# Graph-network kernel on one core: adjacency loads of 2 KB runs over half the row blocks, all from SyncE

## Chip, cores and metric

One core of one Trainium2 chip runs the program. The metric is device time in microseconds (us) of one execution.

## What is computed

`x` is 4096 x 128, `adj` 4096 x 4096 (float32). Two layers are applied; only the parts that matter here are kept:

```python
h = relu(layernorm(x))
# layer 1: z = lap_mul(adj, h) @ W1 + b1, leaky relu; S = exp(-dist(z, z) / 2), 4 best per row kept
#          out = lap_mul(S + adj, h) @ W2 + b2        with lap_mul(A, v) = d * (A @ (d * v)), d = 1/sqrt(rowsum(A))
x = x + out
h = relu(layernorm(x))
# layer 2: x @ Wself.T + (adj @ h) @ Wneigh.T + b
x = x + out2
```

So `adj` (64 MB) multiplies a 4096 x 128 matrix three times: in layer 1 for `z` and again for the output, and in layer 2.

## The kernel before

**Stages.** The first pass over `adj` (to about 504 us) yields row sums and the first product. The distance stage follows (to about 826 us): 16 pairs of row tiles, each with matmuls into eight PSUM banks, key stores to DRAM by SyncE (L411), searches on VectorE, and GpSimd gathers of candidates. The second pass forms `(S + adj)` times the scaled `h` (to about 1158 us). The third pass forms `adj @ h` of layer 2.

**Tiling of passes two and three.** `adj` is cut into 8 groups of rows. A group's rows are 16 row blocks `m` of 32 rows `r`; its 4096 columns are four quarters `q` of 1024. Quarter `q` sits in partitions 32q to 32q+31, one row `r` per partition. The buffer `araw` has 4 slots of 16 KB per partition. Slot `c` takes chunk `c` of a group: 256 columns of each quarter, all 16 row blocks, 2 MB, through four DMAs of 512 KB, one for each quarter. Each DMA moves 512 runs of 1 KB (`load`, L351). A chunk holds 2 of the group's 8 units; a unit is 128 columns of every quarter.

For unit `j`, VectorE transposes 128 x 2048 elements of `araw` in 32 x 32 blocks into `tr[j % 4]` (`product_unit` L1013, instruction at L844), and TensorE multiplies that (L1275): 4 float32 matmuls of 512 columns, which the trace lists as 8. A `tr` buffer is written again when the unit four places earlier was used (semaphore `t_used`), or, for even units of the third pass, split (`lo_done`).

**Third pass.** Odd units go as before. Even units are split into a high and a low part: ScalarE writes the high part of the unit (`split_high`, L780), GpSimd subtracts it (`split_low`, L594), and TensorE then makes 12 matmuls (L1313). TensorE takes the units in order 0 to 7, except in the third pass's group 0, which has no splits and takes even units first (L1342).

**What is woven in.** For each group of the second pass VectorE has three pieces of work: `finish_second_a` of the group before (L1045: adds the gathered rows, layer norm statistics) after unit 6, `finish_second_b` after unit 7, `finish_second_c` of two groups before after unit 3. TensorE does `finish_second_b` after unit 0, `_c` after unit 1, `_a` after unit 2 (L1294). In the third pass VectorE does `finish_third` (L1100) of the group before after unit 3, when TensorE has done its part after unit 0. ScalarE evacuates a group's sum (L729) and stores its result with 4 DMAs (L774) between the splits.

**Who loads.** SyncE issues quarters 0 and 1 (`LOW`, `load_group` L438), ScalarE quarters 2 and 3 (`HIGH`, `load_high` L731, `load_third` L782), among its other instructions. Each issue waits until the slot's units of the group before are transposed (`load_chunk`, L381). The first group's four chunks are issued by SyncE alone, all quarters in the order 0, 1, 2, 3: chunks 0 and 1 between key stores of the distance stage (L422), chunks 2 and 3 at its end (L430, L432). GpSimd gathers 16 x 64 KB per group in the second pass (L553).

Of the kernel before, what the change touches and what calls it, by code (L numbers as in the profile page):

```python
# [41 lines left out]
CHUNKS = GROUPS // CHUNK_UNITS  # L42
SLOTS = 4
# [6 lines left out]
def gnn_kernel(nc, x, adj, W1, b1, W2, b2, W, b, out):  # L50
# [3 lines left out]
    adj_v = adj.rearrange("(m g r) (q c) -> q r g m c", m=QD * U, g=GROUPS, q=QD)  # L54

# [10 lines left out]
    with ctx:  # L66
# [49 lines left out]

        xs_g = xs[:].rearrange("p (u g) f -> p g u f", g=GROUPS)
# [273 lines left out]
        def _(sp):  # L391
# [28 lines left out]
            for n in range(SLOTS // 2):  # L420
                keys_store(1 + n)
                load(sp, n, 0, n * CHUNK_COLS, CHUNK_COLS, ALL)  # L422
# [7 lines left out]
            load(sp, 2, 0, 2 * CHUNK_COLS, CHUNK_COLS, ALL)  # L430
            sp.wait_ge(max_done, TILES // 2)
            load(sp, 3, 0, 3 * CHUNK_COLS, CHUNK_COLS, ALL)  # L432
# [11 lines left out]
            with sp.Fori(1, GROUPS + 1) as g2:  # L444
                load_group(g2)
# [154 lines left out]
        def _(act):  # L600
# [136 lines left out]
            def finish_second(g, last_chunk=True):  # L737
                act.wait_ge(var_ready, g + 2)
                act.activation(tmp32[:, 0:U], tmp32[:, 0:U], ACT.Sqrt).then_inc(sd_done, 1)
                if last_chunk:  # L740
                    load_high(g + 2, 3)
                act.wait_ge(kept, g + 1)
                act.wait_ge(zt_mm, g + GROUPS)
                wait_alone(act, z_done, g + (GROUPS + 1))
                for u in range(U):
                    ins = act.activation(z_st[:, u], xs[:, bass.ds(g + GROUPS * u, 1), :].rearrange("p o f -> p (o f)"), ACT.Relu,
                                         bias=negmr[:, u:u + 1], scale=tmp32[:, u:u + 1])
                ins.then_inc(h2_done, 1)
                act.wait_ge(zt_mm, g + (GROUPS + 1))
                act.wait_ge(q_mm, g + GROUPS)  # L750
                act.activation(flat(t_st[:]), ps_t, ACT.Copy).then_inc(zt_ev, 1)

            def group_second(g, i):
                load_high(g + 1, 0, 1, 2)
                finish_second(g - 1)
                evacuate(g, i, USED1, GROUPS)

            load_high(1, 0, 1, 2, 3)
# [7 lines left out]
            finish_second(GROUPS - 1, False)  # L766
            load_high(GROUPS + 1, 0, 1, 2, 3)
# [8 lines left out]
            def split_high(g, j):  # L776

                act.wait_ge(t_used, g * GROUPS + (USED1 + UNITS + j - 3))
                wait_alone(act, t_ready, g * GROUPS + (UNITS1 + UNITS + j + 1))
                act.activation(tr_hi[:, j // 2 % 2], tr[:, j % TSLOTS], ACT.Copy).then_inc(hi_done, 1)  # L780

            def load_third(g, c):  # L782

                eng_g = g + 1 if isinstance(g, int) else act.snap(g + 1)
                load_chunk(act, g + (GROUPS + 1), eng_g, c, HIGH)

            def group_third(g, i, loads=True):
                split_high(g, 0)
                split_high(g, 2)
                if loads:  # L790
                    load_third(g, 0)
                evacuate(g - 1, 1 - i, USED1 + UNITS, 2 * GROUPS)
                split_high(g, 4)
                if loads:
                    load_third(g, 1)
                store(g - 1, 1 - i)
                split_high(g, 6)
                if loads:
                    load_third(g, 2)
                    load_third(g, 3)  # L800
# [7 lines left out]
            group_third(GROUPS - 1, 1, False)  # L808
# [4 lines left out]
        def _(v):  # L813
# [199 lines left out]
            def product_unit(g, j, base_group, base_unit, place=None, slot_split=None):  # L1013

                place = j if place is None else place
                c, half = divmod(j, CHUNK_UNITS)
                if half == 0:
                    v.wait_ge(a_in[c], (g + base_group + 1) * PER_LOAD + loads_in[c])
# [4 lines left out]
                transposed(tr[:, place % TSLOTS], c, half * UNIT_COLS, U).then_inc(t_ready, 1)  # L1023


            for j in range(2):
                product_unit(0, j, 0, USED1)
# [84 lines left out]
            def group_third(g, i, prev):  # L1112
                for j in range(GROUPS):
                    after_split = j % 2 == 0 and not (isinstance(g, int) and j < TSLOTS)
                    product_unit(g, j, GROUPS, USED1 + UNITS, slot_split=split_units(g, j) - 1 if after_split else None)
                    if j == 2 and isinstance(g, int):
                        finish_second_c(GROUPS - 1)
                    if j == 3:
                        finish_third(prev, 1 - i)
# [7 lines left out]
            for place, j in enumerate(EVENS_FIRST):  # L1127
                product_unit(0, j, GROUPS, USED1 + UNITS, place)
# [13 lines left out]
        def _(pe):  # L1142
# [128 lines left out]
            def unit(g, j, bank, base_unit, src):  # L1271

                pe.wait_ge(t_ready, g * GROUPS + (base_unit + j + 1))
# [20 lines left out]
            def group_second(g, i, prev, before):  # L1294
                pe.wait_ge(acc_read, g + (2 * GROUPS - 2))
                for j in range(GROUPS):
                    if isinstance(g, int) and g == 0:
                        pe.wait_ge(y_ready, GROUPS + j + 1)
                    unit(g, j, i, UNITS1, ys)
# [22 lines left out]
            def group_third(g, i, prev):  # L1322
                pe.wait_ge(acc_read, g + (3 * GROUPS - 2))
                for j in range(GROUPS):
                    if j % 2 == 0:
                        split_unit(g, j, i)
                    else:
                        unit(g, j, i, UNITS1 + UNITS, hs)
# [13 lines left out]
            for place, j in enumerate(EVENS_FIRST):  # L1342
                pe.wait_ge(t_ready, UNITS1 + UNITS + place + 1)
# [41 lines left out]
```

## Time and profile before

| | us |
|---|---|
| median of 3 runs | 1495.37 |
| lowest, highest | 1486.2, 1497.4 |
| the profiled execution | 1488.5 |
| its span in the trace | 1486.7 |

The profiled execution is 6.9 us under the median of the runs, and its span leaves out 1.8 us around it. Times in the rows below are microseconds from the span's start. A line such as `DVE tr L844` is VectorE (DVE), the tensor written, and the code line; ACT is ScalarE, POOL GpSimd, PE TensorE; a `q` behind an engine is its queue or sequencer, as in `SPq` for SyncE. A float32 matmul stands as two in the counts.

### The profile page before, as it was taken

To read this page: it belongs to the slowest core of one execution; us is meant where nothing else is said; L and a number is where in the kernel's file an instruction comes from. 1 tells how busy PE (TensorE), PEld (TensorE's weight loads), DVE (VectorE), ACT (ScalarE), POOL (GpSimd) and SP (SyncE) were. 2 spreads that over 40 slices of the span, in tenths; PEclk is the share of its full clock that TensorE was granted. 3 is DMA by queue.
4 is the path that set the end of the run, shared out by engine and by line. 5 is a ranking of instruction groups with operands and counts; after the bars stand their busy time and mean duration, and the time that the engine had idled before them with its cause. 6 is when DMAs were issued, how large, how long until landed. Compare 5 with 4: busy or idle time off the path is not lost.

```text
span 1486.7 us, 12333 instructions
## 1 busy us (share of the span) xinstructions
PE 1065.4 (72%) x3170; PEld 609.4 (41%) x3170; DVE 871.5 (59%) x888; ACT 406.9 (27%) x997; POOL 475.3 (32%) x572
## 2 busy tenths in 40 slices
PE   0315556689787887899994778878697637878687
PEld 0202222334343366677773333433243314545444
DVE  1514553566655557799997737666465625545453
ACT  0534433554221054455552000000000102222131
POOL 1101111114121023344443175445344014535354
PEclk9956667899899988999997898989799877989899
DMA  9999999999999497443346899999999499999992
GB/s 191 189 222 198 224 211 195 202 223 196 183 198 220 101 217 169 158 168 144 134 174 148 194 237 241 211 248 236 201 253 219 102 206 218 261 230 226 210 232 52
DMA packets 254467, 291.36 MB, mean 196 GB/s; under 512 B 21600, under 2 KB 231520, under 8 KB 254432
## 3 DMA queue, kind: packets, MB, share of 16 engines
q1 hardware_dynamic: 161888, 162.49, 47.5%
q10 hardware_dynamic: 72576, 67.12, 20.1%
q0 software_dynamic: 19968, 61.36, 18.7%
q8 instruction: 13, 0.21, 0.1%
q14 instruction: 22, 0.18, 0.0%
HBM read 251.07 MB, written 39.85 MB: 196 GB/s over the span
## 4 chain that ended last, share of the span: by engine, by line
DMA 19%; DVE 14%; PE 11%; issue 8%; SPq 7%; ACTq 6%; POOL 4%; ACT 2%; DVEq 1%; POOLq 0%
DMA araw<-in_adj_dram 17%; SPq L358 7%; ACTq L358 4%; DVE tr L844 4%; POOL sq_rows L594 2%; PE ps L1313 2%; DVE m L987 2%; ACTq L774 2%; DVE i L989 2%; DVE bmax L974 2%; DMA t_st<-keys_scratch,block_row 2%; DVE out_t L1054 1%; PE ps L1257 1%; PE ps L1275 1%; PE ps L1260 1%
## 5 line engine op out<-in xcount | busy, mean ns | idle before, releaser
L844 DVE STREAM_TRANSPOSE tr<-araw 128x2048 f32<-128x2048 f32 (+3 forms) x244 | 441.6, 1839 | 363.4 <-DMA araw<-in_adj_dram 259.3
L1275 PE MATMUL ps<-tr,ys 128*128 128x512 f32 x512 | 256.2, 658 | 93.6 <-DVE tr L844 55.6
L1164 PE MATMUL ps<-tr,ys 128*128 128x512 f32 x448 | 236.7, 678 | 103.3 <-DVE tr L844 103.3
L358 POOL DMA_DIRECT2D araw<-in_adj_dram x120 | 77.7, 652 | 402.0 <-DVE tr L844 233.7
L1275 PEld LDWEIGHTS ps<-tr,ys 128*128 128x128 f32 x512 | 105.7, 213 | 230.0 <-issue 173.5
L1164 PEld LDWEIGHTS ps<-tr,ys 128*128 128x128 f32 x448 | 93.4, 218 | 221.4 <-issue 144.3
L705 ACT ACTIVATE araw<-ps,nsq 128x1024 f32<-128x1024 f32 x128 | 142.7, 1117 | 128.7 <-PE ps L1260 97.9
L594 POOL TENSOR_TENSOR sq_rows<-tr,zt_lo 128x2048 fp32r<-128x2048 f32 x28 | 126.8, 4536 | 158.2 <-ACT zt_lo L780 158.2
L553 POOL DMA_INDIRECT zt_lo<-neighbour_table,idx_st x128 | 129.8, 1014 | 46.0 <-issue 41.1
L627 ACT ACTIVATE ps<-araw 128x256 f32<-128x256 f32 x304 | 111.1, 366 | 61.4 <-DMA araw<-in_adj_dram 60.9
L1257 PE MATMUL ps<-sq_rows,pick 128*128 128x512 f32 x256 | 103.9, 406 | 26.2 <-POOL zs_lo L470 17.9
L1313 PE MATMUL ps<-sq_rows,zt_hi 128*128 128x512 f32 x112 | 56.8, 507 | 73.9 <-POOL sq_rows L594 73.8
L780 ACT ACTIVATE zt_lo<-tr 128x2048 fp32r<-128x2048 f32 x28 | 53.2, 1912 | 195.6 <-issue 96.4
L1258 PE MATMUL ps<-zt_lo,zs_hi 128*128 128x512 f32 x256 | 102.1, 399 | 0.0
L1259 PE MATMUL ps<-zt_hi,zs_lo 128*128 128x512 f32 x256 | 102.1, 399 | 0.0
L1260 PE MATMUL ps<-zt_hi,zs_hi 128*128 128x512 f32 x256 | 102.1, 399 | 0.0
L1275 PE MATMUL ps<-tr,hs 128*128 128x512 f32 x224 | 100.8, 592 | 0.0
L869 DVE TENSOR_REDUCE part<-araw 128x16 f32<-128x4096 f32 x13 | 57.5, 4420 | 71.8 <-DMA araw<-in_adj_dram 71.8
L1313 PE MATMUL ps<-zt_lo,zt_hi 128*128 128x512 f32 x224 | 81.4, 449 | 0.0
L987 DVE MAX8 m<-araw 128x8 f32<-128x4096 f32 x16 | 70.9, 4430 | 9.3 <-ACT araw L705 8.8
L482 POOL DMA_INDIRECT t_st<-keys_scratch,block_row x64 | 66.6, 1041 | 30.0 <-issue 24.7
L989 DVE FIND_INDEX8 i<-m,araw 128x8 uint32<-128x4096 f32 x16 | 70.7, 4419 | 0.0
(138 smaller groups left out, 1043.8 us busy)
## 6 DMA issues: line engine op xcount, KB each, us to landing
araw<-in_adj_dram SPq DMA_DIRECT2D x200, 512.0 KB
araw<-in_adj_dram ACTq DMA_DIRECT2D x120, 512.0 KB
araw<-in_adj_dram POOLq DMA_DIRECT2D x64, 512.0 KB, 16.0
keys_scratch<-araw SPq DMA_DIRECT2D x64, 512.0 KB, 3.6
xs<-in_x_dram SPq DMA_DIRECT2D x8, 512.0 KB, 7.7
araw<-in_adj_dram POOLq DMA_DIRECT2D x16, 256.0 KB, 8.9
araw<-in_adj_dram SPq DMA_DIRECT2D x16, 256.0 KB
araw<-in_adj_dram POOLq DMA_DIRECT2D x8, 448.0 KB, 10.6
```

What stands on the lines that cost most here:

```text
L358: eng.dma_start(araw[R * q:R * q + R, slot, :, at:at + cols], src).then_inc(landed[slot], DMA)
L553: gp.indirect_dma_start(out=gath[:, i, u, k, :], out_offset=None, in_=table, in_offset=bass.IndirectOffsetOnAxis(ap=idx_st[:, i, u * TOPK ...
L594: gp.tensor_tensor(tr_lo[:, i], tr[:, j % TSLOTS], tr_hi[:, i].bitcast(F32), ALU.subtract).then_inc(lo_done, 1)
L627: act.activation(junk[(m // 2) % 2][:, m % 2 * CHUNK_COLS:(m % 2 + 1) * CHUNK_COLS], araw[:, c, m], ACT.Copy, accum_out=part[:, g % 2, c, ...
L705: act.activation(keys[par][:, c * 1024:c * 1024 + 1024], ps[:, 2 * c:2 * c + 2].rearrange("p a b -> p (a b)"), ACT.Identity, bias=nsq[:, b ...
L844: return v.transpose(out.rearrange("p t (m s) -> p t m s", s=R), src)
L1164: pe.matmul(acc[bank], ys[:, c * GROUPS + first + i], ring1[:, (k + i) % RING1], start=start and i == 0, stop=stop and i == tiles - 1).the ...
L1257: pe.matmul(ps[:, c], pick[:], sq, start=True, stop=False)
L1258: pe.matmul(ps[:, c], zs_hi[:, par], zl, start=False, stop=False)
L1260: ins = pe.matmul(ps[:, c], zs_hi[:, par], zh, start=False, stop=True)
L1275: ins = pe.matmul(acc[bank], src[:, j * U + i], tr[:, j % TSLOTS, i], start=j == 0 and i == 0, stop=j == GROUPS - 1 and i == U - 1)
L1313: ins = pe.matmul(acc[bank], y[:, i, j // 2], t[:, half, i], start=j == 0 and i == 0 and n == 0, stop=False)
```

## The change

In passes two and three slot `n = 2w + h` now takes column half `w` (512 columns of each quarter, units 4w to 4w+3) and row-block half `h` (8 of the 16 row blocks). A slot still holds 2 MB in four DMAs of 512 KB, but each DMA has 256 runs of 2 KB. A unit is complete when its two half transposes, one from slot 2w and one from slot 2w+1, are done. VectorE goes slot by slot: the first halves of units 0 to 3, their second halves, then the same for units 4 to 7. The `finish` pieces move to the ends of slots: `_c` after slot 1, `_a` after slot 2, `_b` after slot 3, `finish_third` after slot 1. SyncE issues all quarters in the order 0, 2, 1, 3, and ScalarE none. The first group's loads keep the order 0, 1, 2, 3.

```diff
+    adj_h = adj.rearrange("(h m g r) (q w c) -> q r g w h m c", h=2, m=QD * U // 2, g=GROUPS, q=QD, w=2)
...
-        def load_chunk(eng, g2, g, c, quarters):
-
-            taken = CHUNKS + c + 1 if isinstance(g2, int) and g2 == GROUPS + 1 else (c + 1) * CHUNK_UNITS
-            eng.wait_ge(t_ready, g2 * GROUPS + (UNITS1 + taken - GROUPS))
-            load(eng, c, g, c * CHUNK_COLS, CHUNK_COLS, quarters)
+        def load_half(eng, n, g, quarters):
+
+            w, h = divmod(n, 2)
+            for q in quarters:
+                if isinstance(g, int):
+                    src = adj_h[q, :, g, w, h]
+                else:
+                    src = adj_h[q, :, bass.ds(g, 1), w, h].rearrange("r o m c -> r (o m) c")
+                eng.dma_start(ahalf[n][R * q:R * q + R], src).then_inc(a_in[n], DMA)
+
+        def load_after(eng, g2, g, n, quarters):
+
+            if isinstance(g2, int) and g2 == 1 and n == 0:
+                taken = HALF_UNITS * 2
+            elif isinstance(g2, int) and g2 == GROUPS + 1:
+                taken = (3 + n // 2) * HALF_UNITS
+            else:
+                taken = (n + 1) * HALF_UNITS
+            eng.wait_ge(t_ready, g2 * STEPS + (UNITS1 + taken - STEPS))
+            load_half(eng, n, g, quarters)
...
                 for c in range(CHUNKS):
-                    load_chunk(sp, g2, g, c, LOW)
+                    load_after(sp, g2, g, c, (0, 2, 1, 3))
...
-            def load_high(g2, *chunks):
-
-                g = g2 % GROUPS if isinstance(g2, int) else g2
-                for c in chunks:
-                    load_chunk(act, g2, g, c, HIGH)
...
+            def half_unit(n, j, place):
+
+                w, h = divmod(n, 2)
+                src = ahalf[n][:, :, (j - w * HALF_UNITS) * UNIT_COLS:(j - w * HALF_UNITS + 1) * UNIT_COLS]
+                dst = tr[:, place % TSLOTS, :, h * (GI // 2):(h + 1) * (GI // 2)]
+                v.transpose(dst.rearrange("p t (m s) -> p t m s", s=R),
+                            src.rearrange("p m (t s) -> p t m s", s=R)).then_inc(t_ready, 1)
...
             def group_second(g, i, prev, before, first=0):
-                for j in range(first, GROUPS):
-                    product_unit(g, j, 0, USED1)
-                    if j == 3 and before is not None:
+                for n in range(SLOTS):
+                    half_landed(n, g, 0)
+                    for j in range(max(first, n // 2 * HALF_UNITS), (n // 2 + 1) * HALF_UNITS):
+                        if n % 2 == 0:
+                            slot_free(g, USED1, j)
+                        half_unit(n, j, j)
+                    if n == 1 and before is not None:
                         finish_second_c(before)
-                    if prev is not None:
-                        if j == 6:
-                            finish_second_a(prev, 1 - i)
-                        if j == 7:
-                            finish_second_b(prev)
+                    if n == 2 and prev is not None:
+                        finish_second_a(prev, 1 - i)
+                    if n == 3 and prev is not None:
+                        finish_second_b(prev)
```

The third pass's `group_third` on VectorE is changed in the same way. TensorE and ScalarE wait for a unit with `unit_ready`, the count of half transposes after its second one. In the third pass's group 0 both halves of a unit are transposed one behind the other, evens first.

## Rows read from the trace of the kernel before

**Rows 1.** The page's part 2: busy share of the DMA engines, 40 slices.

```profile
DMA  9999999999999497443346899999999499999992
```

**Rows 2.** Windows: start:end, length, busy of PE, PEld, DVE, ACT, POOL, PE clock, DMA, GB/s.

```profile
826.00:1158.40 332.40, 267.12 (x640) 120.93 (x640) 204.58 (x294) 19.36 (x47) 149.33 (x156) 0.87 0.97 228
1158.40:1217.10 58.70, 35.18 (x96) 16.77 (x96) 25.91 (x41) 4.26 (x10) 3.69 (x4) 0.83 0.65 145
1217.10:1486.70 269.60, 203.72 (x624) 123.87 (x624) 131.26 (x65) 57.89 (x36) 126.75 (x28) 0.87 0.89 203
```

**Rows 3.** Waits from 860 to 1158 us: us in total, times, longest.

```profile
DVE tr L844 <- DMA araw<-in_adj_dram: 53.3, 12, 17.5
```

**Rows 4.** Waits from 1158 to 1487 us.

```profile
DVE tr L844 <- DMA araw<-in_adj_dram: 88.2, 19, 21.5
PE ps L1313 <- POOL sq_rows L594: 73.8, 18, 23.4
```

**Rows 5.** Timeline of PE: start, length, instructions, [idle before <- released by].

```profile
864.54 5.72 PE L1275 MATMUL ps<-tr,ys 128*128 128x512 f32 x7 [6.98 <-DVE tr L844]
...
1153.13 5.23 PE L1275 MATMUL ps<-tr,ys 128*128 128x512 f32 x8 [4.95 <-DVE tr L844]
```

**Rows 6.** Windows inside two units: columns as in rows 2.

```profile
1126.00:1136.00 10.00, 10.00 (x26) 4.41 (x25) 1.22 (x1) 0.00 (x0) 7.82 (x8) 1.00 0.90 162
1143.00:1147.00 4.00, 4.00 (x6) 1.89 (x7) 3.56 (x14) 0.00 (x0) 0.00 (x0) 0.62 1.03 275
```

**Rows 7.** Timeline of ACT: evacuations of the third pass's groups 6 and 7.

```profile
1449.39 0.58 ACT L729 ACTIVATE out_t<-ps 128x512 f32<-128x512 f32 x1
...
1480.52 0.60 ACT L729 ACTIVATE out_t<-ps 128x512 f32<-128x512 f32 x1 [12.64 <-PE ps L1275]
```

**Rows 8.** Timeline of DVE: finish_second_a, and the third pass's first transposes of group 1.

```profile
930.50 1.08 DVE L1054 SCALAR_TENSOR_TENSOR out_t<-zt_lo,vals,ps 128x128 f32<-128x128 f32 x4
...
938.30 0.17 DVE L1074 TENSOR_SCALAR tmp<-mv 128x4 f32<-128x4 f32 x1
...
1214.86 4.50 DVE L844 STREAM_TRANSPOSE tr<-araw 128x2048 f32<-128x2048 f32 x2 [21.48 <-DMA araw<-in_adj_dram]
```

**Rows 9.** The chain that ended last, third pass's group 7: start, length, what.

```profile
1452.40 4.61 PE ps L1313 x12
1457.01 0.91 PE ps L1150 x8
...
1461.16 1.93 ACT zt_lo L780
...
1463.22 4.56 POOL sq_rows L594
...
1467.83 3.06 PE ps L1313 x12
1470.88 3.43 PE ps L1275 x8
```

**Rows 10.** Groups by line and form: count, busy, mean ns, idle before.

```profile
L844 DVE STREAM_TRANSPOSE tr<-araw 128x2048 f32<-128x2048 f32 x159 | 362.0, 2297 | 285.2 <-DMA araw<-in_adj_dram 203.5 <-issue 39.9 <-PE ps L1275 36.9
...
L844 DVE STREAM_TRANSPOSE tr<-araw 128x1024 f32<-128x1024 f32 x21 | 25.5, 1223 | 26.0 <-DMA araw<-in_adj_dram 26.0
```

**Rows 11.** DMA totals at 651 to 655, 803 to 823, 1230 to 1330 us.

```profile
DMA packets 445, 1.63 MB, mean 407 GB/s; under 512 B 48, under 2 KB 48, under 8 KB 445
...
DMA packets 3259, 3.37 MB, mean 168 GB/s; under 512 B 163, under 2 KB 3195, under 8 KB 3259
...
DMA packets 24573, 23.55 MB, mean 236 GB/s; under 512 B 884, under 2 KB 24569, under 8 KB 24569
```

**Rows 12.** Timeline of DVE in the distance stage: one search starts each pair.

```profile
579.76 4.40 DVE L974 TENSOR_REDUCE bmax<-araw 128x32 f32<-128x4096 f32 x1
...
603.97 4.40 DVE L974 TENSOR_REDUCE bmax<-araw 128x32 f32<-128x4096 f32 x1
619.52 4.40 DVE L974 TENSOR_REDUCE bmax<-araw 128x32 f32<-128x4096 f32 x1
```

More of the change, by code:

```diff
@@ L42 @@
 CHUNKS = GROUPS // CHUNK_UNITS
+HALF_COLS = 2 * CHUNK_COLS
+HALF_UNITS = GROUPS // 2
+STEPS = 2 * GROUPS
 SLOTS = 4
@@ L114, in gnn_kernel @@
         stats4 = sb("stats4", [P, U, 6])
+        ahalf = [araw[:, n].rearrange("p m c -> p (m c)").rearrange("p (m c) -> p m c", c=HALF_COLS) for n in range(SLOTS)]
         xs_g = xs[:].rearrange("p (u g) f -> p g u f", g=GROUPS)
@@ L421, in _ @@
                 keys_store(1 + n)
-                load(sp, n, 0, n * CHUNK_COLS, CHUNK_COLS, ALL)
+                load_half(sp, n, 0, ALL)
             with sp.Fori(1 + SLOTS // 2, TILES // 2) as pair:
@@ L429, in _ @@
             sp.wait_ge(block_maxima, TILES // 2)
[L430 removed]
+            load_half(sp, 2, 0, ALL)
             sp.wait_ge(max_done, TILES // 2)
[L432 removed]
+            load_half(sp, 3, 0, ALL)
             sp.wait_ge(gw_ready, 1)
@@ L441, in load_group @@
                 for c in range(CHUNKS):
-                    load_chunk(sp, g2, g, c, LOW)
-            with sp.Fori(1, GROUPS + 1) as g2:
+                    load_after(sp, g2, g, c, (0, 2, 1, 3))
+            load_group(1)
+            with sp.Fori(2, GROUPS + 1) as g2:
                 load_group(g2)
@@ L1011, in _, with half_landed, slot_free @@
             v.tensor_scalar(vals_f, vals_f, 1e-10, None, ALU.add).then_inc(s_arg, 1)
[L1013 to L1018, printed above, removed]
+            def half_landed(n, g, base_group):
+                v.wait_ge(a_in[n], (g + base_group + 1) * PER_LOAD + loads_in[n])
+            def half_unit(n, j, place):
[4 more added lines that the diff above has]
+                            src.rearrange("p m (t s) -> p t m s", s=R)).then_inc(t_ready, 1)
+            def slot_free(g, base_unit, place, slot_split=None):
                 if slot_split is not None:
@@ L1022, in product_unit @@
                     v.wait_ge(t_used, g * GROUPS + (base_unit + place - TSLOTS + 1))
-                transposed(tr[:, place % TSLOTS], c, half * UNIT_COLS, U).then_inc(t_ready, 1)
-            for j in range(2):
-                product_unit(0, j, 0, USED1)
+            for n in range(2):
+                half_landed(n, 0, 0)
+                for j in range(2):
+                    if n == 0:
+                        slot_free(0, USED1, j)
+                    half_unit(n, j, j)
             v.wait_ge(s_exp, 1)
@@ L1112, in group_third @@
             def group_third(g, i, prev):
[L1113 to L1116, printed above, removed]
+                for n in range(SLOTS):
+                    half_landed(n, g, GROUPS)
+                    for j in range(n // 2 * HALF_UNITS, (n // 2 + 1) * HALF_UNITS):
+                        after_split = j % 2 == 0 and not (isinstance(g, int) and j < TSLOTS)
+                        if n % 2 == 0:
+                            slot_free(g, USED1 + UNITS, j, split_units(g, j) - 1 if after_split else None)
+                        half_unit(n, j, j)
+                    if n == 1 and isinstance(g, int):
                         finish_second_c(GROUPS - 1)
-                    if j == 3:
+                    if n == 1:
                         finish_third(prev, 1 - i)
@@ L1127, in _ @@
             for place, j in enumerate(EVENS_FIRST):
-                product_unit(0, j, GROUPS, USED1 + UNITS, place)
+                slot_free(0, USED1 + UNITS, place)
+                for h in range(2):
+                    n = j // HALF_UNITS * 2 + h
+                    half_landed(n, 0, GROUPS)
+                    half_unit(n, j, place)
                 if place == TSLOTS - 1:
@@ L1298, in group_second @@
                         pe.wait_ge(y_ready, GROUPS + j + 1)
-                    unit(g, j, i, UNITS1, ys)
+                    unit(g, j, i, 0, ys)
                     if j == 0 and before is not None:
@@ L1327, in group_third @@
                     else:
-                        unit(g, j, i, UNITS1 + UNITS, hs)
+                        unit(g, j, i, GROUPS, hs)
                     if prev is not None and j == 0:
@@ L1342, in _ @@
             for place, j in enumerate(EVENS_FIRST):
-                pe.wait_ge(t_ready, UNITS1 + UNITS + place + 1)
+                pe.wait_ge(t_ready, UNITS1 + GROUPS * STEPS + 2 * (place + 1))
                 for i in range(U):
```

34 lines of the change are left out of this document (12 added, 22 removed).

## Prediction, on record before the changed kernel ran

> **What bounds the kernel now.** First the 40 slices: the DMA engines are at nine tenths or more in nearly all slices but those of the distance stage [rows 1]. Then the windows by stage: in the second and third pass DMA is 0.97 and 0.89 busy, at only 228 and 203 GB/s, while PE is busy 80% and 76% of the stretch [rows 2]. Then the waits: VectorE waits for `araw` to land for 53.3 us in pass two and 88.2 us in pass three, and in pass three PE waits 73.8 us for GpSimd's split [rows 3, 4]. So transfers pace these passes, but compute is close behind: that matters more here than the transfers. A thing to fix is each stage's length. Pass two, from the first matmul of group 1 to the last of group 7: 864.5 to 1158.4, 293.9 us, 42 a group [rows 5]. Then 58.7 us to the first transposed unit of pass three's group 1 (the first of a pair begun at 1214.86, so 1217.1) [rows 2, 8]. Then 263.4 us for pass three's groups 1 to 7 [rows 7].
>
> **Transfers.** A group is 16 loads of 512 KB, 8.39 MB. Bytes and DMA count stay; runs double to 2 KB, packets halve, and one queue does what two did. No row shows 2 KB runs. The bounds: SyncE alone with 1 KB runs moved 168 GB/s, both queues 236 GB/s, SyncE's key stores in packets near 4 KB 407 GB/s [rows 11]. Per packet and engine, 168 GB/s is 16 x 1024 B / 168 = 98 ns, and 407 GB/s is 161 ns for 4096 B. On a straight line between them 2048 B take 119 ns, about 275 GB/s. I take 270 GB/s (7.8 us for a 2 MB slot, 31 us a group), as the line from the same queue; the ends 168 and 407 stay for the range. The swapped order 1, 2 gets no term of its own: no row tells it from 0, 1, 2, 3; it lies inside these ends.
>
> Two rules of the Trainium skill bear on this. The page "DMA: Bandwidth & Descriptors", section "Issuing engines are not separate DMA queues", says that several issuing engines share the same 16 DMA engines and save issue time only; by it leaving ScalarE out costs nothing. The rows with 1 KB runs disagree: 236 against 168 GB/s. The same page, "Specifications", puts the line rate from 512 B up, so 2 KB runs would add nothing; that is the second rival below. The 407 GB/s of the long packets speak against it.
>
> **VectorE.** A full transpose takes 2297 ns, one of 128 x 1024 takes 1223 ns [rows 10]. Eight more instructions a group, 16 x 1.22 - 8 x 2.30 = 1.2 us: small, and VectorE is busy 62% in pass two [rows 2]. I use 1.2 us for a half.
>
> **The order, pass two.** Here is the cost. Before, a unit was ready after one transpose, and the four `tr` buffers let VectorE run ahead. Now unit 4 needs its second half from slot 3, behind the first halves of units 4 to 7, and unit 7's first half needs the buffer of unit 3. So when VectorE finishes slot 2, PE has used units 0 to 3 and has nothing. Behind slot 2 stands `finish_second_a`: 930.5 to 938.5, 8.0 us [rows 8]. A group, from the moment unit 0 is ready (0), with transfers never late and PE at 3.43 us a unit [rows 9]: PE ends unit 0 at 3.5, unit 1 at 7.4, unit 2 at 11.7, unit 3 at 16.1 (with its woven pieces, 0.9 us each as the 0.91 in rows 9, the transposes about half that: 2.3 us in all). VectorE writes unit 7's first half at 17.3, ends `finish_second_a` at 25.3, and unit 4 is ready at 26.5. PE stood 10.4 us. After an idle of 5 us a unit took 5.23 us instead of 3.43, at a granted clock of 0.62 in such a unit against 1.00 in a steady stretch [rows 5, 6]; so unit 4 ends at 31.7, unit 7 at 42.0. The next group's last first half waits for unit 7: 43.2, and its unit 0 is ready at 44.4. That idle of 2.4 us may cost a slow unit too (1.8). So 44.4 to 46.2 with a slow unit 4, 42.6 with none; I take 45. Before it was 42. Six groups of 45 and a last one of 44 make 314, against 293.9: +20 us. Transfers need 31 us plus 1.05 MB of gathers, 35 us: hidden. Slot 0 is free when the next group's first halves are done and needed again after VectorE's slot 3, some 32 us later (43.2 to 45 + 30), against 7.8 of transfer.
>
> **The order, pass three.** The same twice a group, with ScalarE and GpSimd in the chain: split 1.93 us, subtraction 4.56, 12 matmuls 3.06 hot and 4.61 after an idle [rows 9]. From unit 0 ready (0): split done 2.0, low part 6.6, unit 0 multiplied at 11.3, `finish_third` on PE 12.4, unit 1 16.0, unit 2 19.0, unit 3 22.6. VectorE waits for PE's 12.4, then slot 2 down to unit 7's first half, which needs unit 3 used: 23.8. Unit 4 ready 25.0, split 27.0, low part 31.6; PE has stood 9 us. Unit 4 ends at 36.3, then 39.8, 42.9, 46.4. Last first half 47.6, next unit 0 ready 48.8. I take 49, and 46 if the slow matmuls did not occur (2 x 1.55 less). Odd units cannot jump ahead: PE takes units in order. ScalarE's stores (four issues) stand between splits of units 4 and 6; unit 6's low part has to be there by 39.8, so up to 6 us of issue are hidden. Six groups of 49 and a last one of 46.5 make 340.5, against 263.4: +77 us. What goes in return is already in this: ScalarE issues no loads between its splits. Transfers need 31 us of 49: hidden.
>
> **Between the passes.** Group 0 of pass three loses its DMA stalls. PE: places 0 to 3 end at 16.4 after pass two's last unit; VectorE finishes `finish_second_a`, `b`, `c` of group 7 at 15 and transposes place 5 by 20, when slots 0 and 1 are free. SyncE issues at once; both slots land after 2 x 7.8 + 2 = 18 us, and unit 0 of group 1 is ready at 40, against 58.7: -19 us. At 168 GB/s it would be 48.
>
> **Distance stage.** Two of its pairs last 24.2 us (579.76 to 603.97) where the next lasts 15.6 [rows 12]: the candidate gather shares the engines with a 2 MB load. A load twice as fast leaves perhaps 7 us less of that. The same holds for the last pair, with slots 2 and 3. I take -14 us for all three; the ends are 0 and -22 (2 x 8.6, and 5).
>
> **Start of pass two.** Group 0 gets two idles of 2.4 us. Group 1's loads can't start early, as ScalarE's could, but stand behind the 2 MB table write in SyncE's queue, and unit 0 now needs two slots. The table and two slots take some 10 + 16 us; so +3 us, from 0 to +10.
>
> **The sum.** -14 + 3 + 20 - 19 + 77 = +67. From 1488.5 us of the profiled execution this is 1555.5; the median of the runs is 6.9 higher, and I give 1558, between the two.
>
> **Rivals.**
> *The transfers set the pace and the order costs little: faster.* For it: 141.5 us of waits for `araw`, and pass three's last group, which had no loads beside it, took 31.1 us instead of 36 [rows 3, 4, 7]. With pass two at 37 a group and pass three at 31: -35 - 38 - 19 - 14 = -106, so 1385. Halfway (40 and 42) it is about 1470, so it decides from idles of under half of what I worked out. Against it: the code leaves PE no unit between slots 2 and 3.
> *The rate stays at 168 GB/s: slower still.* The mechanism is one queue whose engines all read the same narrow column slice. Pass two then needs (8.39 + 1.05 MB) / 168 = 56 us a group, +78 us over 45; pass three 50 against 49, +6; +8 between the passes, +14 in the distance stage, +7 at the start. 1558 + 113 = 1671. For it: SyncE alone at 168 with 1 KB runs. Against: at twice the run it would need 195 ns a packet, more than 4 KB packets took.
> *The slow matmuls don't occur and the loads gain fully.* Pass two 42.6, pass three 46, distance stage -22: -16 - 20 - 8 = -44 on the forecast, about 1514.
> *It cancels:* near 1495, if order and transfers each come out by half.
>
> **How the numbers follow.** A measurement of this kernel tells about 1% from no change. Forecast, order-bound: 0.65. No slow matmuls: 0.13. Rate stays: 0.09. Cancels: 0.06. Faster: 0.07. So faster by over 1% 0.07, within 1% 0.07, slower 0.86. The range 1505 to 1620 leaves out the faster cases, the cancelled one and most of the stayed rate, and takes in partial rates of 190 GB/s and the forecast's own 1525 to 1590.
>
> **What would show it.** In pass two the wait of `PE L1275` for `DVE tr` grows to about 10 us once a group, behind L1074, and groups last 45 us with DMA far under 0.9 busy. In pass three groups last 49 us, with two idles of 8 to 9 us on PE before L1313, released by `sq_rows L594`. Waits for `araw` nearly vanish. Pairs of the distance stage with loads last about 17 us, and the gap of 58.7 us becomes 40. It is wrong if groups of pass three last under 42 us, or if `araw` still ends most of VectorE's waits.

## Result, and the profile after

| | before | after |
|---|---|---|
| median of 4 runs in one comparison, us | 1496.38 | 1563.18 |
| lowest, highest | 1486.2, 1501.78 | 1554.95, 1569.47 |
| profiled execution, its span | 1488.5, 1486.7 | 1566.38, 1564.6 |

The ratio is 1.0452, with a 95% interval of 1.0396 to 1.0508: slower by 67 us, where 1558 had been forecast. The two spans differ by 77.9 us, and the stages below account for that.

The page of after: the DMA shares of the 40 slices, the chain by engine, and the groups of the transposes and of the matmuls that wait for them.

```profile
DMA  9999999999998585433378999999994998888850
PE 37%; DVE 14%; DMA 8%; POOL 6%; issue 5%; ACT 3%; SPq 1%; DVEq 1%; POOLq 0%; ACTq 0%
L1025 DVE STREAM_TRANSPOSE tr<-araw 128x1024 f32<-128x1024 f32 x256 | 300.7, 1220 | 243.1 <-PE ps L1298 191.3
L1336 PE MATMUL ps<-sq_rows,zt_hi 128*128 128x512 f32 x112 | 61.7, 551 | 136.6 <-POOL sq_rows L621 136.6
```

The shares stay high through pass two and fall to about eight tenths in pass three [rows 1]. The transposes' idle is now ended by PE and not by `araw` [rows 10]. Windows of after, columns as in rows 2:

```profile
818.04:864.30 46.26, 34.30 (x65) 14.22 (x65) 28.53 (x26) 0.60 (x1) 19.29 (x21) 0.83 0.81 183
864.30:1183.00 318.70, 231.66 (x578) 106.17 (x579) 186.24 (x336) 19.50 (x47) 131.95 (x138) 0.85 1.01 217
1183.00:1226.40 43.40, 31.31 (x97) 15.41 (x94) 26.41 (x49) 3.56 (x9) 1.85 (x2) 0.93 0.55 113
1226.40:1564.60 338.20, 207.87 (x624) 129.24 (x624) 130.48 (x116) 57.45 (x36) 126.70 (x28) 0.79 0.77 166
```

The second row is pass two's groups 1 to 7, the third the stretch between the passes, the fourth pass three's groups 1 to 7 and an end of 6.2 us, which before was as long. Of the span's +77.9 us, the start of pass two comes 7.8 us earlier (818.0 for 825.8), group 1 comes 7.5 us later than that allows (864.3 - 818.0 = 46.3, against 38.7), pass two takes 24.8 us more (318.7, 293.9), the stretch between the passes 15.3 us less (43.4, 58.7), and the third pass 68.6 us more (332.0, 263.4). That sums to 77.8.

Waits of after from 860 to 1190 us, and then from 1190 us to the end, to be set beside rows 3 and 4:

```profile
PE ps L1298 <- DVE tr L1025: 94.4, 14, 10.5
DVE tr L1025 <- PE ps L1298: 84.0, 41, 3.2
DVE tr L1025 <- DMA araw<-in_adj_dram: 12.1, 3, 5.4
```

```profile
PE ps L1336 <- POOL sq_rows L621: 136.6, 14, 18.0
DVE tr L1025 <- PE ps L1298: 100.2, 26, 6.8
```

PE's wait for the split nearly doubled (73.8 before), and in pass two the 53.3 us for `araw` fell to 12.1, while PE and VectorE now wait for each other in turn. The three waits in those 12.1 us stand in group 1 (to 873 us) and behind the last group (1183 us); between them VectorE never waits for a load, although the DMA engines' share of pass two is 1.01, where the prediction had expected far under 0.9. The timeline of PE shows how, in pass two and in pass three:

```profile
1011.91 3.60 PE L1298 MATMUL ps<-tr,ys 128*128 128x512 f32 x8
1025.89 15.41 PE L1298 MATMUL ps<-tr,ys 128*128 128x512 f32 x32 [10.38 <-DVE tr L1025]
1043.77 3.70 PE L1298 MATMUL ps<-tr,ys 128*128 128x512 f32 x8 [2.46 <-DVE tr L1025]
...
1305.27 0.80 PE L1336 MATMUL ps<-sq_rows,zt_hi 128*128 128x512 f32 x1 [9.12 <-POOL sq_rows L621]
1328.60 0.79 PE L1336 MATMUL ps<-sq_rows,zt_hi 128*128 128x512 f32 x1 [9.12 <-POOL sq_rows L621]
```

Once a group PE has multiplied unit 3 and stands 10.38 us until unit 4 has its second half (x32 is units 4 to 7), then 2.46 us until the next unit 0. In pass three it stands 9.12 us twice a group, always the same; idles that repeat like that point to a cycle between engines and not to transfers. The long wait of pass two has `finish_second_a` in it, as the timeline of VectorE shows, 927.24 to 935.30:

```profile
927.24 1.08 DVE L1066 SCALAR_TENSOR_TENSOR out_t<-zt_lo,vals,ps 128x128 f32<-128x128 f32 x4
...
935.13 0.17 DVE L1086 TENSOR_SCALAR tmp<-mv 128x4 f32<-128x4 f32 x1
935.21 4.62 DVE L1025 STREAM_TRANSPOSE tr<-araw 128x1024 f32<-128x1024 f32 x4
```

DMA totals of after, at 900 to 1180 us, and the GB/s of 1200 to 1226 us in 40 slices, where nothing but loads runs at the end:

```profile
DMA packets 31034, 60.25 MB, mean 215 GB/s; under 512 B 3179, under 2 KB 3179, under 8 KB 31028
...
GB/s 0 0 0 0 66 180 183 170 164 132 151 139 142 173 303 258 224 202 176 227 249 230 224 227 227 224 230 221 221 233 221 233 214 239 211 224 227 239 211 227
```

With 2 KB runs and nothing beside it the one queue levels off near 225 GB/s. The forecast had 270.

### The profile page after: what moved, and what is told of

Read it like the earlier page. It is cut to its first block, busy times and chain, and to the rows that moved or that the text cites. A ratio compares the mean times of both kernels' runs of the same rounds, so it can differ in the third digit from the quotient of the medians.

```text
span 1564.6 us, 12488 instructions
## 1 busy us (share of the span) xinstructions
PE 1056.3 (68%) x3170; PEld 607.4 (39%) x3170; DVE 880.8 (56%) x1016; ACT 405.6 (26%) x997; POOL 475.8 (30%) x572
## 4 chain that ended last, share of the span: by engine, by line
PE 37%; DVE 14%; DMA 8%; POOL 6%; issue 5%; ACT 3%; SPq 1%; DVEq 1%; POOLq 0%; ACTq 0%
PE ps L1298 21%; DMA araw<-in_adj_dram 7%; PE ps L1336 7%; POOL sq_rows L621 4%; DVE tr L1025 4%; DVE m L991 2%; DVE out_t L1066 2%; DVE i L993 2%; ACT zt_lo L796 2%; DVE bmax L978 2%; PE ps L1187 2%; PE ps L1280 2%; PE ps L1281 1%; PE ps L1282 1%; PE ps L1283 1%
## 5 line engine op out<-in xcount | busy, mean ns | idle before, releaser
L1025 DVE STREAM_TRANSPOSE tr<-araw 128x1024 f32<-128x1024 f32 x256 | 300.7, 1220 | 243.1 <-PE ps L1298 191.3
L848 DVE STREAM_TRANSPOSE tr<-araw 128x512 f32<-128x512 f32 (+3 forms) x116 | 150.5, 1333 | 137.6 <-DMA araw<-in_adj_dram 111.8
L363 POOL DMA_DIRECT2D araw<-in_adj_dram x120 | 77.8, 653 | 400.1 <-DVE tr L848 295.6
L1336 PE MATMUL ps<-sq_rows,zt_hi 128*128 128x512 f32 x112 | 61.7, 551 | 136.6 <-POOL sq_rows L621 136.6
L1336 PEld LDWEIGHTS ps<-sq_rows,zt_hi 128*128 128x128 f32 x112 | 27.4, 245 | 156.3 <-POOL sq_rows L621 129.3
L1336 PE MATMUL ps<-zt_lo,zt_hi 128*128 128x512 f32 x224 | 85.0, 467 | 0.0
## 6 DMA issues: line engine op xcount, KB each, us to landing
araw<-in_adj_dram POOLq DMA_DIRECT2D x64, 512.0 KB, 15.3
```

The costliest lines, as they stand in the source:

```text
L848: return v.transpose(out.rearrange("p t (m s) -> p t m s", s=R), src)
L1025: v.transpose(dst.rearrange("p t (m s) -> p t m s", s=R), src.rearrange("p m (t s) -> p t m s", s=R)).then_inc(t_ready, 1)
L1336: ins = pe.matmul(acc[bank], y[:, i, j // 2], t[:, half, i], start=j == 0 and i == 0 and n == 0, stop=False)
```

## Experiments

Two theories stood against each other. *Order:* the halves leave PE no ready unit between slots 2 and 3, and the time is the cycle in which PE and VectorE wait for each other. *Transfers:* 2 KB runs from one queue bring the data too late. The runs stand in three groups that share their runs of the kernel before, median 1491.34 us for experiments 1 to 3, 1483.64 for 4, 5 and 8, 1502.47 for 6, 7 and 9. A ratio is always to the kernel before of the same group.

**1. No loads.** From the changed kernel, and from the kernel before, the loads of groups 1 to 7 of pass two and all of pass three are left out; the old contents of the slots are multiplied again.

```diff
-            load_group(1)
-            with sp.Fori(2, GROUPS + 1) as g2:
-                load_group(g2)
...
             def half_landed(n, g, base_group):
-                v.wait_ge(a_in[n], (g + base_group + 1) * PER_LOAD + loads_in[n])
+                if isinstance(g, int) and g == 0 and base_group == 0:
+                    v.wait_ge(a_in[n], PER_LOAD + loads_in[n])
```

> The changed kernel without the loads of groups 1 to 7 of pass two and of all of pass three (the old slot contents are multiplied again, so the transfers cost nothing). Theory: the changed kernel is bound by its order of halves. Then a group of pass two still lasts 44.5 to 46 us and one of pass three 47.8 us; only the waits for slots at the start of pass two (some 10 us) and between the passes (some 12 us) go, about 1540 us in all. Rival: the single queue of loads binds it. Then groups fall towards 37 and 31 us, and the time towards 1400 us.

> The kernel before without the same loads. Theory: there the transfers bind and the order costs little, so groups fall from 42 to 32 to 36 us in pass two and from 36.5 to about 31 us in pass three, and the stall between the passes goes: 1370 to 1390 us. Rival: compute was as close behind as in the changed kernel; then it stays above 1450 us.

Measured, one execution each: 1567.99 us for the changed kernel, 1296.24 us for the kernel before. The windows of both, changed kernel first (passes two and three each, columns as in rows 2):

```profile
863.00:1180.00 317.00, 227.50 (x552) 103.76 (x551) 181.26 (x330) 18.45 (x44) 137.08 (x143) 0.83 0.09 24
1227.00:1560.00 333.00, 206.19 (x616) 128.25 (x616) 131.32 (x117) 56.87 (x35) 126.41 (x28) 0.79 0.02 6
```

```profile
864.00:1100.00 236.00, 234.94 (x661) 113.02 (x660) 203.22 (x319) 25.48 (x57) 146.60 (x153) 1.00 0.13 34
1105.00:1290.00 185.00, 182.17 (x624) 112.10 (x624) 124.83 (x61) 53.43 (x34) 123.48 (x27) 1.00 0.04 10
```

The DMA engines are nearly idle in the first fence, and the kernel is no faster than with its loads (1554.95 to 1569.47). PE's timeline has the same cycle:

```profile
1006.28 5.40 PE L1293 MATMUL ps<-tr,ys 128*128 128x512 f32 x8 [2.46 <-DVE tr L1020]
1034.59 16.97 PE L1293 MATMUL ps<-tr,ys 128*128 128x512 f32 x32 [10.38 <-DVE tr L1020]
1054.02 5.40 PE L1293 MATMUL ps<-tr,ys 128*128 128x512 f32 x8 [2.46 <-DVE tr L1020]
```

So the time of the changed kernel's passes is set by the order of its work, with the lower clock that goes with its idles, and not by its transfers. The expected gain of some 25 us did not come, because here every group of pass two from the second on had the slow first unit (5.40 us for 3.70 and 16.97 for 15.41), 47.7 us a group for 44.5. The kernel before was bound by transfers: without them PE is busy without a gap at a granted clock of 1.00, 29.7 us a group in pass two and 26.2 in pass three. I had taken compute to be much closer behind. Of the changed kernel's 18 us more a group part is the clock: a matmul takes 227.50 / 552 = 412 ns in its pass two, 234.94 / 661 = 355 ns in the other.

**2. The new loads in the old order of units.** Slots of 2 KB runs, one queue, 0, 2, 1, 3, but VectorE makes both halves of a unit one behind the other. With that, the `finish` pieces go back to where the kernel before had them, and slots 2w and 2w + 1 come free together.

```diff
+            def whole_unit(g, j, base_group, base_unit, slot_split=None):
+                slot_free(g, base_unit, j, slot_split)
+                for h in range(2):
+                    n = j // HALF_UNITS * 2 + h
+                    if j % HALF_UNITS == 0:
+                        half_landed(n, g, base_group)
+                    half_unit(n, j, j)
...
             def group_second(g, i, prev, before, first=0):
-                for n in range(SLOTS):
...
+                for j in range(first, GROUPS):
+                    whole_unit(g, j, 0, USED1)
```

> The changed kernel's loads (2 KB runs, one queue), but VectorE completes unit after unit, both halves one behind the other, and the finish pieces stand where they stood before; slots are freed two at a time. Theory: the order costs all of the loss in pass three and the transfers, at the 217 to 228 GB/s of the changed kernel's trace, then bind: 9.44 MB / 217 = 43.5 us a group in pass two, 8.39 MB / 228 = 37 us in pass three, 1563 - 7 x 1.5 - 7 x 10.8 = 1477, within 1465 to 1500. Rival: halves as such, or freeing late, cost as much as the order: above 1540 us.

Measured: 1495.84 us (1486.19 to 1511.29), ratio 1.0015, 0.9981 to 1.005: the time of before. The waits of 860 to 1170 us, and the DMA totals of 1240 to 1400 us:

```profile
DVE tr L1021 <- DMA araw<-in_adj_dram: 112.6, 18, 11.6
PE ps L1291 <- DVE tr L1021: 78.7, 21, 14.1
```

```profile
DMA packets 20957, 37.05 MB, mean 232 GB/s; under 512 B 1352, under 2 KB 3400, under 8 KB 20953
```

The order of halves, with the places of the `finish` pieces that go with it, costs all of the loss, 67 us. The rest of the change, longer runs and one queue for two, comes to nothing here. And this kernel is bound by transfers again: VectorE waits for `araw`, at 220 to 232 GB/s, which is what two queues with 1 KB runs had (228 in pass two, rows 2). It is not the most that one queue of 2 KB runs can carry: experiment 8, where slots come free one at a time, moves 240 GB/s. Whether freeing them in pairs costs the difference was not tried.

**3. The order of the quarters.** The changed kernel with 0, 1, 2, 3.

```diff
-                    load_after(sp, g2, g, c, (0, 2, 1, 3))
+                    load_after(sp, g2, g, c, ALL)
```

> The changed kernel with SyncE's quarters in the order 0, 1, 2, 3. Theory: bound by the order of halves, it does not feel the order of quarters: within 0.5% of the changed kernel, 1555 to 1571 us, and the rate of the loads in a stretch full of them changes by under 5%. Rival: the swap keeps both halves of the partitions busy; without it the rate falls well under 217 GB/s, pass two becomes transfer-bound, and the time is over 1600 us.

Measured: 1560.82 us (1553.55 to 1576.0), ratio to before 1.0466 (1.0391 to 1.0541): the changed kernel's own. As this kernel is bound by its order of halves, the time alone couldn't show a slower queue; the rate can. DMA totals from 900 to 1100 us, this run first, then the changed kernel:

```profile
DMA packets 23070, 44.81 MB, mean 224 GB/s; under 512 B 2488, under 2 KB 2488, under 8 KB 23067
DMA packets 22621, 43.95 MB, mean 220 GB/s; under 512 B 2371, under 2 KB 2371, under 8 KB 22617
```

In one queue the order of quarters with 2 KB runs makes no difference to either.

**4. One queue with 1 KB runs.** The kernel before, with all quarters from SyncE, in the order 0, 1, 2, 3 and in the order 0, 2, 1, 3.

```diff
                 for c in range(CHUNKS):
-                    load_chunk(sp, g2, g, c, LOW)
+                    load_chunk(sp, g2, g, c, ALL)
...
-                for c in chunks:
-                    load_chunk(act, g2, g, c, HIGH)
+                return
```

> The kernel before (1 KB runs, chunk order) with all quarters from SyncE in the order 0, 1, 2, 3 and none from ScalarE. Theory: with 1 KB runs one queue moves 168 GB/s as between 803 and 823 us of the trace before, so a group takes 9.44 MB / 168 = 56 us in pass two and 8.39 / 168 = 50 us in pass three, about 1491 + 7 x 14 + 7 x 13.5 = 1684 us. Rival: the number of queues doesn't matter and ScalarE's freed issue time helps; then 1470 to 1495 us.

> As the run before (1 KB runs, one queue), but quarters in the order 0, 2, 1, 3. Theory: as with 2 KB runs the order of quarters makes no difference: within 1% of the run with 0, 1, 2, 3. Rival: neighbouring loads that fall on the two halves of the partitions overlap better; then at least 3% faster than 0, 1, 2, 3.

Measured: 1665.23 us, ratio 1.1231 (1.1143 to 1.1319), and 1732.22 us, ratio 1.1667 (1.1592 to 1.1742). DMA totals from 900 to 1100 us, each kernel's own:

```profile
DMA packets 35137, 36.77 MB, mean 184 GB/s; under 512 B 1884, under 2 KB 34262, under 8 KB 35133
```

```profile
DMA packets 32148, 33.65 MB, mean 168 GB/s; under 512 B 1728, under 2 KB 31343, under 8 KB 32144
```

So run length and queues each matter: 2 KB runs repair what the second queue's loss would cost. SyncE's issues of loads in the first of these kernels, 1240 to 1400 us (shortest, median and longest in ns), speak against issue time as the reason:

```profile
L358 SPq DMA_DIRECT2D araw<-in_adj_dram x46: 322/2745/7778, 1238.7 to 1399.3; - x46
```

An issue that nothing holds up takes 0.32 us, so the 16 of a group take 5 us. The median of 2.7 us would fit a queue that is full and takes the next load late; why it moves no more is open.

The Trainium skill's page "DMA: Bandwidth & Descriptors" puts the line rate from 512 B up ("Specifications"). One queue with the quarters in plain order disagrees: 184 GB/s with 1 KB runs, 224 with 2 KB (experiment 3). The same page's section "Issuing engines are not separate DMA queues" says that a second issuing engine saves only issue time. Here the second queue was worth 12% of the kernel's time.

That the order 0, 2, 1, 3 is slower than 0, 1, 2, 3 with 1 KB runs, by 67 us, was not expected, and its cause stays open.

**5. Two queues with 2 KB runs.** Experiment 2's kernel, with quarters 0 and 1 from SyncE and 2 and 3 from ScalarE, as before.

```diff
-                    load_after(sp, g2, g, c, (0, 2, 1, 3))
+                    load_after(sp, g2, g, c, LOW)
...
             def group_second(g, i):
+                load_high(g + 1, 0, 1)
                 finish_second(g - 1)
```

> Unit by unit as in the third run, 2 KB runs, but quarters 2 and 3 from ScalarE as before. Theory: runs and queues add up (one queue 168 with 1 KB and 217 to 228 with 2 KB, two queues 236 with 1 KB), so the rate rises to some 280 GB/s, groups fall to 34 to 37 us and the time to 1420 to 1450 us. Rival: at 225 to 236 GB/s the transfers have met a limit that neither runs nor queues move; then 1480 to 1505 us.

Measured: 1429.72 us (1423.68 to 1441.82), ratio 0.9667 (0.9581 to 0.9754), faster than both kernels. GB/s from 1150 to 1190 us, one slice a microsecond:

```profile
GB/s 0 0 0 0 0 0 0 0 0 0 0 0 0 0 0 0 0 137 182 164 188 248 219 217 209 219 207 217 211 238 354 360 336 352 360 336 352 360 322 236
```

SyncE alone moves 207 to 219 GB/s, and when ScalarE's loads join, 322 to 360 flow. That is a peak: from 900 to 1100 us the mean is 244 GB/s.

**6. The same with both queues on one half of the partitions.** SyncE issues quarters 0 and 2, ScalarE 1 and 3, so that the two queues work at 0 and 1, then at 2 and 3. As its counterpart, the kernel before with that split.

```diff
-                    load_after(sp, g2, g, c, LOW)
+                    load_after(sp, g2, g, c, (0, 2))
...
-                    load_after(act, g2, g, n, HIGH)
+                    load_after(act, g2, g, n, (1, 3))
```

> As the seventh run (unit by unit, 2 KB runs, two queues; 1429.7 us, stretches at 305 to 360 GB/s), but SyncE takes quarters 0 and 2 and ScalarE 1 and 3, so that what is in flight together lies mostly in one half of the partitions (0 to 63, then 64 to 127). Theory: the plateau of 217 to 228 GB/s of one queue belongs to one quarter's partitions, that is to the 8 of 16 SBUF ports that partitions 0 to 63 or 64 to 127 reach (the Trainium skill, page SBUF, puts 0 to 63 at some 218 GB/s and 128 partitions at 436); then this split loses most of the gain, stretches with both queues stay mostly under 250 GB/s and the time is 1470 to 1500 us. Rival: two queues give more for being two, whatever they write; then it stays within 1% of 1430 us.

> The kernel before (1 KB runs, two queues), with SyncE on quarters 0 and 2 and ScalarE on 1 and 3. Theory: the two queues paid for being on two halves of the partitions; together on one half the rate falls from 227 towards the 184 GB/s of one queue with 1 KB runs, so 1540 to 1660 us. Rival: with 1 KB runs the limit is in the packets, not in the half; then within 1.5% of the kernel before.

Measured: 1484.56 us, ratio 0.9864 (0.9789 to 0.994), and 1554.9 us, ratio 1.0332 (1.0231 to 1.0433). The first kernel's GB/s from 1150 to 1190 us; the second one's wait for `araw` from 860 to 1200 us:

```profile
GB/s 215 217 223 221 205 221 236 213 203 209 215 231 209 215 203 225 229 203 215 201 117 18 0 0 0 0 0 0 0 0 0 0 0 0 0 0 0 0 0 25
```

```profile
DVE tr L844 <- DMA araw<-in_adj_dram: 126.7, 22, 28.6
```

With two queues at work, each moving half of it, the rate is back at 201 to 236 GB/s. So with 2 KB runs the plateau goes with the half of the partitions that is written, and not with the queue. One rival is left: in this layout a quarter's partitions and its columns of `adj` go together, so these runs can't tell the written half from the columns that are read at the same time.

The Trainium skill's page "SBUF — State Buffer", section "Door 1: The DMA port swizzle", has partitions 0 to 63 share eight of sixteen ports, with an asymptote of 218 GB/s. The trace agrees in size. The same page's "Can I just issue two DMAs to hit both halves?" says that two of them at once gain 6% only. The trace disagrees, with 207 to 219 GB/s becoming 322 to 360.

With 1 KB runs the same split costs 3.3%, as the time had been forecast, but the rate did not fall towards the 184 GB/s of one queue. DMA totals of 900 to 1100 us:

```profile
DMA packets 41850, 44.41 MB, mean 222 GB/s; under 512 B 2517, under 2 KB 40517, under 8 KB 41846
```

The kernel before has 227 there. So with 1 KB runs the half is the smaller part of what one queue lacks.

**7. Two queues in the order of halves.** The changed kernel with quarters 0 and 1 from SyncE, 2 and 3 from ScalarE.

```diff
-                    load_after(sp, g2, g, c, (0, 2, 1, 3))
+                    load_after(sp, g2, g, c, LOW)
...
+                load_high(g + 1, 0, 1, 2)
                 finish_second(g - 1)
```

> The changed kernel with its order of halves, but quarters 2 and 3 from ScalarE again. Theory: bound by the order of halves, it gains nothing in pass three (47.8 us a group) and little in pass two: 1545 to 1565 us, though the loads are fast. Rival: faster loads pay here too; then under 1500 us.

Measured: 1568.6 us (1558.91 to 1575.5), ratio 1.0468 (1.0405 to 1.0531). PE's timeline, with 44.47 us from one unit 0 to the next (47.8 later in pass two, as in the changed kernel):

```profile
988.46 3.70 PE L1321 MATMUL ps<-tr,ys 128*128 128x512 f32 x8 [2.46 <-DVE tr L1048]
1015.07 15.40 PE L1321 MATMUL ps<-tr,ys 128*128 128x512 f32 x32 [10.38 <-DVE tr L1048]
1032.93 3.70 PE L1321 MATMUL ps<-tr,ys 128*128 128x512 f32 x8 [2.46 <-DVE tr L1048]
```

The second queue that gains 3.5% in the order of units (ratio 0.9667 for 1.0015, experiments 5 and 2) gains nothing in that of halves.

**8. `finish_second_a` one slot earlier.** VectorE does it after slot 1, ahead of slot 2's first halves and while PE still has units 0 to 3; PE's part moves from after unit 2 to after unit 0.

```diff
+                    if n == 1 and prev is not None:
+                        finish_second_a(prev, 1 - i)
                     if n == 1 and before is not None:
                         finish_second_c(before)
-                    if n == 2 and prev is not None:
-                        finish_second_a(prev, 1 - i)
```

> The changed kernel with finish_second_a ahead of slot 2 instead of behind it (and PE's part of it after unit 0). Theory: its 8 us stood between PE's units 3 and 4 and are now covered by units 1 to 3; PE's idle there falls from 10.4 to about 4 us. Alone that is 7 x 6.3 = 44 us, but at 217 GB/s the transfers then need 43.5 us a group, so pass two gains 15 to 30 us and the time is 1530 to 1548 us. Rival: the transfers already paced pass two; then nothing is gained, 1555 us or more.

Measured: 1536.78 us (1529.0 to 1544.2), ratio 1.0379 (1.0306 to 1.0452). PE's timeline in pass two:

```profile
1019.07 5.19 PE L1298 MATMUL ps<-tr,ys 128*128 128x512 f32 x8 [2.46 <-DVE tr L1025]
1025.95 1.15 PE L1173 MATMUL ps<-w2s,out_t 128*128 128x128 f32 x8 [1.25 <-ACT out_t L756]
1041.70 15.70 PE L1298 MATMUL ps<-tr,ys 128*128 128x512 f32 x32 [3.40 <-DVE tr L1025]
```

The wait before unit 4 falls from 10.4 to 3.4 us and a group from 44.5 to some 41 us; pass three stays at 47.8 to 48.2 a group. So `finish_second_a` behind slot 2 made 7.0 us of the 10.4. The group gains less than those 7.0, as PE now waits 1.25 us for ScalarE's `out_t` and unit 0 is the slow one (5.19 us for 3.70). The expectation had transfers stop the gain at 43.5 us a group; they did not, and the one queue, with the gathers beside it, brings more than in any other run here. DMA totals of 900 to 1100 us:

```profile
DMA packets 24713, 47.97 MB, mean 240 GB/s; under 512 B 2512, under 2 KB 2512, under 8 KB 24709
```

The two profiled spans differ by 37 us, but the ratios to before only by 0.0073, some 11 us, with intervals that overlap: the size of the gain over the whole kernel is not settled by these runs.

**9. ScalarE's loads earlier.** Experiment 5's kernel, with ScalarE's loads of slots 0 and 1 for pass three's group 1 ahead of its wait for PE at the end of pass two.

```diff
                 ins.then_inc(h2_done, 1)
+                if not last:
+                    load_high(GROUPS + 1, 0, 1)
                 act.wait_ge(zt_mm, g + (GROUPS + 1))
...
-            load_high(GROUPS + 1, 0, 1, 2, 3)
+            load_high(GROUPS + 1, 2, 3)
```

> The seventh run, with ScalarE's loads of slots 0 and 1 for pass three's group 1 issued ahead of its wait for PE's transposes; there SyncE's queue ran alone at 217 GB/s for some 8 us. Theory: both slots land some 6 us earlier, 1420 to 1427 us. Rival: PE or the GpSimd chain is late there anyway; then no change.

Measured: 1415.81 us (1414.78 to 1433.12), ratio 0.9469 (0.9388 to 0.9551), the best of all. Its lead over experiment 5's kernel is 14 us by the medians and 2% by the ratios, each to its own runs of the kernel before. In the profiles the first split unit of pass three's group 1 is multiplied at 1195.28 us, for 1201.30 in experiment 5, which is the 6 us that were expected.

## Why the prediction was right

The time (1558 forecast, 1563.18 measured) came out, and so did the mechanism of its two largest terms, the order of halves. That the number is within 5 us is in part luck. The sum of +67 us was made from the profiled execution of before, and profile against profile it is +77.9: every term but pass three was too low or its gain too high, by 19 us together, and pass three was 8 too high. The two profiled executions lie on opposite sides of their medians, which brings the difference of the medians back to 67. By its own steps:

- **The order, pass two.** Right, and shown by experiments 1, 2 and 8: PE runs dry between slots 2 and 3. "PE stood 10.4 us": 10.38. The idle of 2.4 us before unit 0: 2.46. A group of 45: 44.5 to 44.9 in three groups running, 47.8 in the sixth. The term was +20 and is +24.8. Mis-sized was "44.4 to 46.2 with a slow unit 4": the slow unit after the 2.46 us idle comes and goes (3.70 or 5.40 us) and the block of units 4 to 7 goes with it (15.4 or 17.0), so the upper end is 47.8.
- **The order, pass three.** Right: groups of 47.8 for 48.8 worked out and 49 taken, idles of 9.12 for 9. The term was +77 and is +68.6. The 1.2 us by which 49 is too long, 1.0 of it in the working and 0.2 in the rounding, make 7 us of the difference over six groups.
- **Transfers.** The step that failed. "A straight line between them" gave 119 ns for 2048 B and 275 GB/s; measured was a plateau near 225, 146 ns. The line ran from loads that write one half of the partitions at a time to key stores that don't, and experiments 5 and 6 show that with 2 KB runs the half (or the columns that go with it) is the limit. It cost the forecast little in the passes, because loads at the lower rate were still hidden: 8.39 MB at 225 GB/s take 37 us of pass two's 44.5, and experiment 8 ran groups of 41 us on the same queue. The low end was off too: one queue with 1 KB runs moves 184 GB/s in experiment 4, where the 168 came from 20 us of the distance stage with a gather of candidates in them.
- **"DMA far under 0.9 busy".** This sign did not come: the share of pass two is 1.01. The busy share doesn't tell whether transfers bind; the waits for `araw` do.
- **"Compute is close behind".** Wrong for the kernel before: without loads it takes 1296 us, so compute was 195 us behind. The order of halves is what brought compute in front. The forecast didn't rest on it, since it built its cycle from durations.
- **Between the passes.** -19 forecast, -15.3 measured, and **start of pass two** +3 forecast, +7.5 measured. In both PE waits for two slots, and 4.19 MB at 225 instead of 270 GB/s take 3 us longer; the other 1.4 us at the start were not traced. At the start VectorE waits for slots 0 and 1 of group 1 to land, in its timeline twice:

```profile
850.64 2.37 DVE L1025 STREAM_TRANSPOSE tr<-araw 128x1024 f32<-128x1024 f32 x2 [5.91 <-DMA araw<-in_adj_dram]
...
862.89 3.50 DVE L1025 STREAM_TRANSPOSE tr<-araw 128x1024 f32<-128x1024 f32 x3 [4.68 <-DMA araw<-in_adj_dram]
```

- **Distance stage.** -14 forecast, -7.8 measured. The prediction has both of its two pairs with a load at 24.2 us. They last 23.8 and 24.2 (the line of before first) and now 18.8 and 19.8, where a pair without a load takes 15.5; 17 was expected. That is -9.4, and the last pair, up to the first matmul of pass two, is 3.9 shorter; a start of the stage 2.4 us later and the other pairs, 3.1 us longer together, take 5.5 back.

```profile
555.97 4.41 DVE L974 TENSOR_REDUCE bmax<-araw 128x32 f32<-128x4096 f32 x1
```

```profile
577.19 4.40 DVE L978 TENSOR_REDUCE bmax<-araw 128x32 f32<-128x4096 f32 x1
597.01 4.40 DVE L978 TENSOR_REDUCE bmax<-araw 128x32 f32<-128x4096 f32 x1
612.55 4.40 DVE L978 TENSOR_REDUCE bmax<-araw 128x32 f32<-128x4096 f32 x1
```

**The rivals.** *Transfers set the pace* falls with experiment 1. Its picture of the kernel before was right, and with the order out of the way and the second queue back its time is nearly reached (1416 for 1385). Its sum has a slip: pass three at 31 us a group is 217 us for 263.4, so -46 and not -38. *The rate stays at 168* falls with the 225 GB/s and 220 to 240 in pass two. *No slow matmuls* held for unit 0 in part of pass two, and nowhere for unit 4. *It cancels* would have needed the order to cost half.

## What to carry to other kernels

When a unit of work is cut so that its parts arrive in different buffers, count when units become complete, not when bytes arrive: with a ring of four buffers and eight units in two rounds, TensorE ran dry each round, and no transfer could mend that (experiments 1 and 7). Take a finer slot only if the consumer can still finish unit by unit; here the same slots in unit order cost nothing, and opened the way to 5% less. For strided loads into few partitions look at run length, number of queues and which partitions are written at the same moment together: longer runs bought with the second queue brought nothing (experiment 2), with all three right the kernel took 1430 us for 1484, and 1416 for 1502 with ScalarE's loads issued earlier.

## What the runs showed of the hardware

- One queue of loads into 32 partitions each levels off at 207 to 239 GB/s with 2 KB runs (220 to 240 with the gathers of pass two beside it), whatever the order of the quarters; two queues on opposite halves of the partitions reach 322 to 360, two on the same half 201 to 236.
- With 1 KB runs one queue moves 184 GB/s, and in the order 0, 2, 1, 3 only 168; two queues move 227, and 222 on the same half. Why is open.
- In a cycle that repeats to 0.1 us, the first unit after the same idle of 2.46 us takes 3.70 us in some groups and 5.40 in others, and stays so for several groups; the same kernel without loads had 5.20 to 5.40 in every group from the second on. What decides it was not tried.
